# Two attention and MLP layers on one core: weight loads behind their splits, earlier next rows and value weights, stores by tile, new places for the MLP pieces

## The reference

```
xn = layernorm(x)
x  = x + attention(xn) + mlp(xn)          # twice, with other weights
attention: q, k = rope(xn Wq^T), rope(xn Wk^T);  v = xn Wv^T      # 16 heads of 32
           softmax(causal(q k^T / sqrt(32))) v, then Wo^T
mlp:       (silu(xn Wg^T) * (xn Wu^T)) Wd^T                       # hidden 2048, then 1408
```

## Time and profile before

| | us |
|---|---|
| median of 3 runs | 1997.6 (1992.91 to 1997.8) |
| profiled execution | 1996.87 |
| its span | 1995.2 |
| TensorE busy | 1846.7 |
| ScalarE busy | 1091.1 |
| VectorE busy | 1067.9 |
| GpSimd busy | 720.2 |
| mean granted TensorE clock | 0.966 |

### The profile page before, as it was taken

The page is one execution under the profiler, slowest core; times in us unless marked ns, Lnnn a source line. Parts: engine busy times, 40 slices in busy tenths (PEclk is TensorE's granted clock), DMA queues, the critical chain, the costliest instruction groups (busy, mean ns, idle before and its releaser), DMA issues.

```text
span 1995.2 us, 24662 instructions
## 1 busy us (share of the span) xinstructions
PE 1846.7 (93%) x8656; PEld 1350.9 (68%) x8656; DVE 1067.9 (54%) x2368; ACT 1091.1 (55%) x2445; POOL 720.2 (36%) x628
## 2 busy tenths in 40 slices
PE   5999999999998999999989989999998889999988
PEld 4777767676776576756467767777776755767564
DVE  5546556472545374737346474555536544646462
ACT  2565657574246484747426556565732554757572
POOL 4234343432433244424133252435334334343331
PEclk9999999999999899999889989999999989999999
DMA  6213121220131121203142031214112212121201
GB/s 221 54 43 90 44 80 44 74 82 23 62 80 49 43 73 52 82 20 114 64 132 75 23 101 43 69 44 122 43 32 69 74 33 80 44 80 38 64 12 42
DMA packets 66122, 130.32 MB, mean 65 GB/s; under 512 B 7504, under 2 KB 8528, under 8 KB 64976
## 3 DMA queue, kind: packets, MB, share of 16 engines
q1 hardware_dynamic: 66000, 128.75, 22.0%
HBM read 73.67 MB, written 4.19 MB: 39 GB/s over the span
## 4 chain that ended last, share of the span: by engine, by line
PE 72%; DVE 11%; ACT 7%; POOL 4%; issue 3%; DMA 2%; SPq 0%; DVEq 0%; POOLq 0%; ACTq 0%
PE D L940 17%; PE G L940 12%; PE U L940 10%; PE OE L1038 7%; PE OE L940 7%; PE SS L1022 6%; PE SS L940 5%; PE OE L1022 3%; PE OE L1001 3%; PE SS L1001 3%; DVE xres L909 2%; POOL wgl L715 2%; ACT OE L636 2%; DVE OE L867 1%; ACT pr L655 1%
## 5 line engine op out<-in xcount | busy, mean ns | idle before, releaser
L909 DVE TENSOR_TENSOR xres<-D,xres 128x512 f32<-128x512 f32 x352 | 238.6, 688 | 262.5 <-PE D L940 259.6
L655 ACT ACTIVATE pr<-SS 128x512 f32<-128x512 f32 (+3 forms) x512 | 233.7, 498 | 148.8 <-PE SS L1022 147.7
L747 POOL TENSOR_TENSOR hl<-tt,hh 128x512 fp32r<-128x512 f32 x108 | 139.2, 1289 | 376.7 <-ACT hh L673 376.3
L636 ACT ACTIVATE OE<-OE,mp 128x384 f32<-128x384 f32 (+3 forms) x256 | 203.9, 798 | 102.4 <-DVE mp L867 101.6
L867 DVE CUSTOM_DVE_ANT_0 OE<-OE,mask 128x384 f32<-128x384 f32 (+3 forms) x256 | 220.5, 873 | 59.1 <-PE OE L1001 57.5
L765 POOL TENSOR_SCALAR_AFFINE_SELECT pr<-pr 128x512 f32<-128x512 f32 x128 | 81.3, 638 | 379.7 <-ACT pr L655 379.6
L1022 PE MATMUL SS<-QS,KS 98*128 98x512 f32 (+2 forms) x512 | 178.0, 395 | 18.8 <-DMA QS<-mt 11.4
L940 PE MATMUL G<-xh,wgh 128*128 128x512 f32 x432 | 178.4, 413 | 16.0 <-DVE tt L920 8.5
L636 ACT ACTIVATE SS<-SS,mp 128x128 f32<-128x128 f32 (+3 forms) x256 | 162.1, 634 | 51.7 <-DVE mp L867 50.2
L867 DVE CUSTOM_DVE_ANT_0 SS<-SS,mask 128x128 f32<-128x128 f32 (+3 forms) x256 | 169.7, 676 | 32.8 <-PE SS L1001 32.3
L940 PE MATMUL D<-wdh,hh 128*128 128x512 f32 x432 | 174.8, 405 | 9.3 <-DVE xres L909 4.5
(11 more groups left out here) (123 smaller groups left out, 3760.8 us busy)
## 6 DMA issues: line engine op xcount, KB each, us to landing
KS<-pr SPq DMA_DIRECT2D x128, 192.0 KB, 3.3
QS<-pr SPq DMA_DIRECT2D x128, 192.0 KB, 3.3
raw<-in_wgate_dram SPq DMA_DIRECT2D x27, 512.0 KB, 3.6
raw<-in_wup_dram SPq DMA_DIRECT2D x27, 512.0 KB, 3.6
raw<-in_wdown_dram SPq DMA_DIRECT2D x27, 512.0 KB, 3.7
raw<-in_wqk_dram SPq DMA_DIRECT2D x16, 512.0 KB, 3.5
trig<-in_wv_dram SPq DMA_DIRECT2D x4, 1024.0 KB, 7.2
trig<-in_rope_dram SPq DMA_DIRECT2D x4, 1024.0 KB, 5.2
```

The lines of the kernel that those rows point to most:

```text
L636: act.activation(s, s, ACT.Exp, bias=mp[:, c, at:at + 1], scale=-1.0, accum_out=se[:, c, at:at + 1]) \
L655: act.activation(weights(i)[:, h, skip:W], SB[(i * HG + h) % 3][:, skip:W], ACT.Exp, scale=-1.0) \
L747: pool.tensor_tensor(hl[:, fc, :], tt[:, (blk * nfc + fc) % 2, :], hh[:, fc, :].bitcast(F32), ALU.subtract) \
L909: dve.tensor_tensor(xres[:, rt, :], d[:, :], xres[:, rt, :], ALU.add).then_inc(sem["v_dfree"], 1)
```

## The change

The step list changes in five ways, and the table of places is new as a whole.

1. A split no longer loads. `loads` walks through a finished layer and puts a step ("load", kind) behind each split, at most eight steps later, or ahead of the next split that uses the same slot. The load waits for its own split's low half. `SLOT` and `SLOTS` move up in the file.
2. `x_next` is two steps of 1024 KB: the first half behind the item that ends in pv(7) of the last turn, the second behind the last pv. The statistics of the first four rows stand behind the four output additions.
3. `v_weights` stands behind the last `heads`, ahead of the output tiles.
4. `store` writes one tile of 128 rows (256 KB) behind each last addition, so 8 transfers for each batch.
5. In `opening`, values(4) stands between norm(6) and norm(7) instead of behind norm(7).

```diff
-    items += [[("pv", n - 2), ("pv", n - 1), ("heads", 1)] + [("x_next",)] * (l == 1 and not final)] + output(1)
+    items.append([("pv", n - 2), ("pv", n - 1), ("heads", 1)] + [("v_weights", 1 - l)] * (not final))
+    items += output(1)
+    if l == 1 and not final:
+        halves = [k for k, it in enumerate(items) if ("pv", TPC * 2 - 1) in it]
+        items[halves[-1]].append(("x_next", 0))
+        items[-TPC - 1].append(("x_next", 1))
+        for rt in range(TPC):
+            items[rt - TPC].append(("row", 0, rt))
+        items[-1] += normal(0)
...
-        items[-3].append(("v_weights", 1))
     else:
-        d0[-1].append(("store", 0))
-        d1[-1].append(("store", 1))
+        for c, d in enumerate((d0, d1)):
+            for i, piece in enumerate(d):
+                piece.append(("store", c * TPC + i))
...
-            items += [[("row", 0, rt) for rt in range(TPC)] + normal(0)] + norms(0, range(TPC))
-            items[-3].append(("v_weights", 0))
+            items += norms(0, range(TPC))
...
+def loads(steps):
+
+    out, due = [], []
+    for x in steps:
+        while due and (due[0][0] <= len(out) or x[0] == "w" and SLOT[x[1]] in [SLOT[kind] for _, kind in due]):
+            out.append(("load", due.pop(0)[1]))
+        out.append(x)
+        if x[0] == "w":
+            due.append((len(out) + BEHIND, x[1]))
+    return out + [("load", kind) for _, kind in due]
...
-    out += values[2:4] + later[0] + [proj[1]] + later[1] + later[2] + later[3] + [("keep", 1)] * (layer == 0) + [values[4]]
+    out += values[2:4] + later[0] + [proj[1]] + later[1] + later[2] + [values[4]] + later[3] + [("keep", 1)] * (layer == 0)
...
-            def w(n, kind):
+            def load_next(n, kind):
                 follows = n.follows(SLOT[kind])
                 if follows:
-                    sp.wait_ge(sem["g_lo"], n("g_lo", 1))
+                    sp.wait_ge(sem["g_lo"], n.ready(kind))
                     load(sp, *follows, raw[:, SLOT[kind], :], f"raw{SLOT[kind]}")
 
-            def store(n, c):
+            def store(n, rt):
                 sp.wait_ge(sem["v_dfree"], n("v_dfree"))
-                sp.dma_start(rows(out, n, c, n.b), xres[:, c * TPC:(c + 1) * TPC, :]).then_inc(sem["d_out"], 16)
+                sp.dma_start(out[n.b, rt * P:(rt + 1) * P, :], xres[:, rt, :]).then_inc(sem["d_out"], 16)
```

In the new table all sixteen strings differ. Two of them, turn 0 and turn 3 of the second layer, first batch:

```diff
-        ("01020030101000101123032011160213021020010110100000000000000000000000000000000000000000000000000000000",
+        ("00013101010010102023053022121121111011001101001000000000000000000000000000000000000000000000000000030",
...
-         "00100020001011100022020311221121110000000000000000000000000000000000000000000000000000000000101026000"),
+         "0010002001001200020210200121204000101000000000000000000000000000000000000000000000000000000010105220"),
```

More of the change, by code:

```diff
@@ L54 @@
 RING = 4
-TILES = True
+BEHIND = 8
+SLOT = {"A": 2, "O": 2, "U": 0, "G": 1, "D": 1}
+SLOTS = 3
 DIGITS = "0123456789abcdefghijklmnopqrstuvwxyzABCDEFGHIJKLMNOPQRSTUVWXYZ"
@@ L236, in layer @@
     first, items, pieces = plan(b, l)
-    return first + paced(items, pieces, PACE[b][l])
+    return loads(first + paced(items, pieces, PACE[b][l]))
+def loads(steps):
[7 more added lines that the diff above has]
+    return out + [("load", kind) for _, kind in due]
 def opening(layer):
@@ L255 @@
     (
[L256 to L259, removed]
-        ("01020030101000101123032011160213021020010110100000000000000000000000000000000000000000000000000000000",
-         "00300030001001010113031112111112121020021001000000100010000100200001000010000000000000000000000000000",
-         "00400011010101010113031203020212121020110100100000110010000101000000000000000000000000000000000000000",
-         "00100020001011100022020311221121110000000000000000000000000000000000000000000000000000000000101026000"),
-    ),
@@ L265 @@
-    (
[L266 to L273, removed]
+        ("01300020100100011012030202111212021020010010020000110101000101000001000010100000010010000011000000000",
+         "00200020101011002003020311130213021020010110100000110010002100100000000010010000010020200010000000020",
+         "20100011000101011004201211111212121020110100100000110010000101000001000101001000001003000101000000010",
+         "00100020101100111013030202111212021020010012000000110101000101000001000010100000010010000011703q0211"),
@@ L285 @@
     "keep": {},
-    "x_next": {"d_x0": 16, "d_x1": 16},
+    "x_next": {},
+    "load": {},
     "xn": {"v_xn": 1},
@@ L314 @@
 STACKS = 16
-SLOT = {"A": 2, "O": 2, "U": 0, "G": 1, "D": 1}
-SLOTS = 3
 SPLITS_OPEN = "ADGU"
@@ L361, in follows @@
     def follows(self, slot):
-        later = SPLITS[slot][self.taken[slot] + 1:]
+        later = SPLITS[slot][self.taken[slot]:]
         return later[0][:2] if later else None
@@ L385, in did @@
         if step[0] == "x_next":
-            self.batches += 1
+            self.batches += step[1] == 0
+            self.n[f"d_x{step[1]}"] += 16
         if step[0] in ("add_wo", "add_down"):
@@ L571, in keep, with x_next @@
                 sp.dma_start(xres[:, c * TPC:(c + 1) * TPC, :], rows(x, n, c, n.batches)).then_inc(sem[f"d_keep{c}"], 16)
-            def x_next(n):
+            def x_next(n, c):
                 sp.wait_ge(sem["p_pv"], n("p_pv"))
[L575 to L578, removed]
+                sp.dma_start(val[:, c * TPC:(c + 1) * TPC, :], rows(x, n, c, n.b + 1)).then_inc(sem[f"d_x{c}"], 16)
             def rotate(n, t):
@@ L595, in flip @@
                                  mt[k * HG * TPC:(k + 1) * HG * TPC, c, :].bitcast(F32)).then_inc(sem["d_shift"], 16)
-            def w(n, kind):
+            def load_next(n, kind):
                 follows = n.follows(SLOT[kind])
                 if follows:
-                    sp.wait_ge(sem["g_lo"], n("g_lo", 1))
+                    sp.wait_ge(sem["g_lo"], n.ready(kind))
                     load(sp, *follows, raw[:, SLOT[kind], :], f"raw{SLOT[kind]}")
-            def store(n, c):
+            def store(n, rt):
                 sp.wait_ge(sem["v_dfree"], n("v_dfree"))
-                sp.dma_start(rows(out, n, c, n.b), xres[:, c * TPC:(c + 1) * TPC, :]).then_inc(sem["d_out"], 16)
-            walk(dict(v_load=v_load, v_weights=v_weights, keep=keep, x_next=x_next, rotate=rotate, flip=flip, w=w, store=store))
-            sp.wait_ge(sem["d_out"], CREDIT["d_out"] + 16 * NC * B)
+                sp.dma_start(out[n.b, rt * P:(rt + 1) * P, :], xres[:, rt, :]).then_inc(sem["d_out"], 16)
+            walk(dict(v_load=v_load, v_weights=v_weights, keep=keep, x_next=x_next, rotate=rotate, flip=flip, load=load_next, store=store))
+            sp.wait_ge(sem["d_out"], CREDIT["d_out"] + 16 * RT * B)
         @block.scalar
```

10 lines of the change are left out of this document (added).

## The result

The changed kernel takes 1915.95 us (median of 4 executions, 1909.38 to 1918.65), the kernel before 1996.35 in executions beside it. The ratio is 0.9595, 95% interval 0.9566 to 0.9624. The profiled execution took 1917.4 with a span of 1915.6, 79.6 less than that of before. The time lies outside the predicted range (1932 to 1980).

The account below looks back on a forecast made before the run. TensorE, busy 93% of the span, was taken as the bound, so only shortening its chain pays. Six gains, 16.2 + 12.1 + 6.6 + 2.4 + 6.6 + 3 = 46.9 us, took 1996.9 to 1950, range 1932 to 1980.

Parts of the forecast that it names:

- A: Second layers' turn 0: loads as steps behind splits let the second flip's transfers leave earlier; 16.2 us gained (0 to 23).
- B: Four openings: twelve values(4) matmuls fill the 2.3 us wait before the last transpose; 12.1 us gained (6 to 12.8).
- C: Batch border: early next rows, statistics between additions and moved value weights shorten TensorE's waits; 6.6 us gained (-3 to 9.8).
- D: Layer borders: reordered fillers and the value copy moved off VectorE's subtractions; 2.4 us gained (0 to 5).
- E: Tail: output tiles fill the last down stage's wait, full clock behind it, smaller last store; 6.6 us gained (1 to 8).
- F: New table of places, all sixteen turns: fewer gate-split waits, 3 us gained; natural tiles nothing, bounded by 20 either way.
- waits of 1.2, 0.5 and 1.4: Batch border: TensorE waits in us expected to remain because VectorE becomes late freeing the two D banks; 3.2 taken off.
- R2: Rival, chance 0.08: SyncE reaches loads with unfinished splits, so flips wait again and the load gain is lost; 1966 us.
- R1: Rival, chance 0.20: idle gaps go but thin stretches stay at the slow clock; 33.0 us gained, 1964.
- R3: Rival: new places thin out natural tiles, opening 2.3 us gaps; 2014 us, chance 0.09; 11 to 13 gaps, within 0.3%, 0.05.

## Why the prediction was wrong, step by step

| term | predicted | shown |
|---|---|---|
| A loads | 16.2 | 15.8 alone, 19.1 in the changed kernel |
| B values(4) | 12.1 | 10.9 alone |
| C batch border | 6.6 | -1.3 with the old table, 8.8 with the new; 2.5 of B are in both |
| D layer borders | 2.4 | 4.4 (segments, old table, beyond B's) |
| E tail | 6.6 | 2.3 from the store, nothing measurable from the order |
| F places | 3 | 48.6 in the new structure, 39.4 alone |

**F is the step that failed**, as a term far too small: 3 us, where the new table was worth 48.6. "I take nothing for that, and bound it by 20 either way" looked only at TensorE's waits for ScalarE and only at one sum of fillers over all turns. The single strings show something else: 14.7 for one (9.2 of them in the border segment), 3.8 for another, nothing for a third, and 25.6 for the eight of the first layers. The 4.8 us that may be chance are in two of these numbers, so 48.6 - (14.7 + 3.8 + 25.6 - 4.8) = 9.3 is left for the five strings of the second layers that were not tried by themselves. The sum of fillers says nothing, because a gap is closed by the piece that lies in front of it.

What there was to win could be counted in the trace of before. Beyond the first 30 us it has 30 gaps of 1.2 us and more, 66.1 us in all. 12 of them, 35.5 us, are those that A to E name; 30.6 us in 18 gaps were left for the table, each with a low clock that may follow. With the old table in the new structure 24 gaps with 47.6 us stand, with the new table 17 with 29.3. So the table closed 18.3 us of such gaps and 8.7 of smaller ones, and 21.6 us of matmul time went with them. In the trace of the changed kernel 12 of its 14 stretches at the low clock begin within 2.1 us of the end of one of the 17 gaps. That ties the clock to the gaps by place; the part of the 21.6 us that is chance was not measured.

The stated range had a slip of its own. The upper ends of A to E add up to 58.6, and F's own bound of 20 brings that to 78.6, that is 1918. The 1936 and the 1932 left most of that bound out, so the range did not hold what F itself allowed, and the measured 1916 lies just beyond even that. C has a small slip too: waits of 1.2, 0.5 and 1.4 are 3.1, not 3.2.

**A** was right in place, size and in its witness: no wait for QS<-mt above 0.3, transfers 0.03 us behind the copy. R2 is out. In the changed kernel it guards five flips instead of two, since the new places alone put three more behind splits. **B** was right. **C** came near in size (8.8 less B's 2.5 against 6.6), by luck, and was wrong in cause: early rows are worth next to nothing (0.3), the value weights' place 1.5, the statistics' 3.1, and with the string of before all of them together gave nothing; the waits of 1.2, 0.5 and 1.4 came as 0.8 and 0.7. The failed thought is that the rows were what was late. With the old string the chunk in front of them is, and TensorE then waits for VectorE's product. **D** had its sign; its parts were not tried alone. **E** counted the 12 matmuls as a gain without asking where they came from: they were taken out of stages that stayed as long. Only the store's 1.0 was there, as 2.3. **R1** did not come about, but a low stretch stayed in the last turn, from 1853 on, where fillers are thin. **R3** had the right lever with the wrong sign: the places decide more than all the rest, and with the table seven gaps fewer stand (24 to 17) instead of 12 more.

The Trainium skill (DMA: Bandwidth & Descriptors, Measured) wants transfers of at least 1 MiB. The loss of about 2 us that the prediction estimated beside this rule counts four fixed costs of 2 us and no time for the data. No run here shows a loss: 256 KB landed in 2.1 us and the end came 2.3 earlier than with 1024 KB.

**Open:** which of the eight first-layer strings carries how much, how the structure and the table share the 8.8 of the batch border, and what decides whether turn 3 runs with 10 or with 31 us at the low clock when its code is the same (92.4 and 98.3 us long).

## What to carry to other kernels
A table that places filler work is not noise to be bounded by one engine's waits: list the bounding engine's gaps above a microsecond, whatever they wait for, take their sum and the low clock behind them as what it can win or lose, and look at each string's pieces in front of each gap. Fillers are conserved, so filling a wait with one of them wins only if its old place could do without it, and a piece that needs another engine's result can stand in the gap it was to fill. Of a wait in an in-order transfer queue ask who is queued behind it, and ask it again after every reordering.

## What the runs showed of the hardware
I had priced a microsecond at the low clock at half a microsecond. Over the whole change 32.1 us of busy time went with 79 us of low time, 0.41 each, and in the last turn, with the same code, 3.6 us of length with some 10 of low time, about a third. Doubling matmuls in a thin stretch changed nothing in the total (0.9605 and 0.9603 against 0.9595). In the changed kernel's trace 12 of the 14 half-speed stretches stand at a gap of 1.4 to 2.4 us. The batch border's old string alone brought 4.9 us of idle time back and 9.8 us of slower matmuls (busy 1824.4 against 1814.6), of which up to 4.8 may be chance: one piece of code took 92.4 us in one kernel and 98.3 in another, with nothing in it changed, at a mean clock of 0.94 and 0.84. Two small transfers stood 3.8 us behind their data because the queue ahead of them waited for another engine, and TensorE paid 5.8 us for it.
